# Moving the first batch's token turns and router products between two blocks of an attention and mixture-of-experts kernel

## The reference

```
x = x + LN(attention(LN(x)))
x = x + LN(ffn(LN(x)))

attention: qkv = x @ w_qkv, 16 heads of 8 channels
  scores = q k^T / sqrt(8), causal mask, + head_scale * q_proj * k_proj
  out = softmax(scores) v @ w_out
ffn: logits = x @ router_w^T over 7 experts; top 2 by value, softmax of the two
  expert(x) = (silu(x @ w_gate) * (x @ w_up)) @ w_down, hidden width 512
  out = sum over the two chosen experts of weight * expert(x) + shared expert(x)
```

## Time and profile before

| | us |
|---|---|
| median of 3 runs | 510.47 |
| the profiled execution | 510.59 |
| span of the profile, first to last instruction | 508.9 |
| PE busy | 421.5 (83%) |
| DVE busy | 337.0 (66%) |
| ACT busy | 247.2 (49%) |
| POOL busy | 185.3 (36%) |

### The profile page before, as it was taken

The page is one execution under the profiler, slowest core; times in us unless marked ns, Lnnn a source line. Parts: engine busy times, 40 slices in busy tenths (PEclk is TensorE's granted clock), DMA queues, the critical chain, the costliest instruction groups (busy, mean ns, idle before and its releaser), DMA issues. The chain is left out here.

```text
span 508.9 us, 10326 instructions
## 1 busy us (share of the span) xinstructions
PE 421.5 (83%) x3468; PEld 237.3 (47%) x3468; DVE 337.0 (66%) x1133; ACT 247.2 (49%) x432; POOL 185.3 (36%) x341
## 2 busy tenths in 40 slices
PE   1745999999999999999999688979699989899600
PEld 0421122333333333333333455646699989899600
DVE  2975988999898989898938636794133222233267
ACT  1430147777777777787878167342222123123230
POOL 9100021423323232415141125345256655664322
PEclk9995559999999999999999679999799989999955
DMA  3066364202011010000000081004267756667152
GB/s 109 1 166 172 91 194 127 64 3 56 11 32 34 9 58 2 3 3 3 3 2 1 0 246 44 3 0 149 83 225 212 210 164 211 205 221 229 64 166 83
DMA packets 43944, 46.55 MB, mean 91 GB/s; under 512 B 5683, under 2 KB 32692, under 8 KB 43892
## 3 DMA queue, kind: packets, MB, share of 16 engines
q1 hardware_dynamic: 41460, 40.91, 27.0%
q0 software_dynamic: 2432, 4.99, 3.5%
HBM read 34.80 MB, written 10.88 MB: 90 GB/s over the span
## 5 line engine op out<-in xcount | busy, mean ns | idle before, releaser
L590 ACT ACTIVATE probs<-banks 128x1024 f32<-128x1024 f32 (+2 forms) x192 | 151.7, 809 | 37.4 <-PE banks L437 35.5
L425 PE MATMUL banks<-k_st,q_st 48*128 48x512 bf16 (+3 forms) x384 | 121.8, 358 | 14.0 <-DMA k_st<-k_rows 11.5
L344 POOL TENSOR_SCALAR_AFFINE_SELECT probs<-probs 128x256 f32<-128x256 f32 x128 | 52.2, 408 | 141.9 <-ACT probs L590 141.1
L455 PE MATMUL banks<-probs,v_pad 128*32 128x256 f32 (+1 forms) x1280 | 97.0, 375 | 1.9 <-ACT o_cols L601 1.0
L437 PE MATMUL banks<-q_st,k_st 51*128 51x512 bf16 (+3 forms) x384 | 93.4, 335 | 3.5 <-DVE mx_part L716 1.3
L716 DVE TENSOR_REDUCE mx_part<-banks 128x1 f32<-128x512 f32 x128 | 77.6, 679 | 5.7 <-PE banks L425 5.7
L1463 DVE TENSOR_TENSOR hidden<-banks,gate 128x512 f32<-128x512 f32 x38 | 26.3, 692 | 65.0 <-ACT gate L1231 25.9
L722 DVE CUSTOM_DVE_ANT_0 scratch<-banks,mask_qk,mx_part 128x384 f32<-128x384 f32 (+3 forms) x128 | 63.9, 548 | 5.5 <-PE banks L425 5.5
L722 DVE CUSTOM_DVE_ANT_0 scratch<-banks,mask_qk 128x512 f32<-128x512 f32 (+3 forms) x128 | 56.2, 486 | 13.7 <-PE banks L425 12.5
L425 PEld LDWEIGHTS banks<-k_st,q_st 48*128 48x128 bf16 x384 | 32.1, 94 | 58.1 <-DVE mx L722 20.1
L437 PEld LDWEIGHTS banks<-q_st,k_st 51*128 51x128 bf16 x384 | 23.5, 94 | 69.9 <-issue 39.1
(11 more groups left out here) (190 smaller groups left out, 460.3 us busy)
## 6 DMA issues: line engine op xcount, KB each, us to landing
w_g<-in_w_gate SPq DMA_DIRECT2D x38, 256.0 KB
w_u<-in_w_up SPq DMA_DIRECT2D x38, 256.0 KB
q_rows<-parts SPq DMA_DIRECT2D x24, 128.0 KB, 2.4
k_rows<-parts SPq DMA_DIRECT2D x24, 128.0 KB, 2.4
q_st<-q_rows SPq DMA_DIRECT2D x32, 96.0 KB, 2.3
k_st<-k_rows SPq DMA_DIRECT2D x32, 96.0 KB, 2.3
w_d<-in_w_down SPq DMA_DIRECT2D x8, 256.0 KB, 4.8
back<-results SPq DMA_DIRECT2D x8, 256.0 KB, 5.0
```

Source lines behind the costliest of these rows:

```text
L344: nc.gpsimd.affine_select(out=part, in_=part, compare_op=ALU.is_ge, fill=0.0, base=0, pattern=[[0, 2], [1, P]], channel_multiplier=-1).the ...
L425: nc.tensor.matmul(max_bank[m % RING][:, 0:width], q_st[r][rows, c, p, (i % CH) * P:(i % CH + 1) * P], k_st[r][rows, kc, p, 0:width], star ...
L455: last = nc.tensor.matmul(o_bank[h * HQ:(h + 1) * HQ, lo:hi], v_pad[:, n, j, h, :], probs[unit % PROBS][:, h, lo:hi], start=(x in FIRST_UN ...
L590: return nc.scalar.activation(probs[unit % PROBS][:, 2 * p:2 * p + 2, first:BANK], slot_pair[p].rearrange("p (a t) -> p a t", a=2)[:, :, 0 ...
```

## The change

NEWTON goes from 4 to 3. In the last group the projection of the first batch is issued behind unit 3 instead of unit 4. The first block's token turns, x2_t copies, router products and logits copy are gone (`first_turn_tokens`, `first_route` and their banks and semaphore). DVE inverts the first half of the last group's sums ahead of writing x2 and the second half right behind it. In the second block PE turns chunk 0 behind its attention turns, then projects, then turns chunk 1; DVE copies both at the head of its list, ahead of its wait for the projection. The router products of chunks 0 and 1 follow shared_up of chunk 0. One copy takes all logits.

```diff
--- before.py
+++ after.py
@@ -43,7 +43,7 @@
 MINUS_ONES = float(np.array([0xBF80BF80], np.uint32).view(np.float32)[0])
 EPS = 1e-5
 RSQRT_BITS = float(0x5F3759DF)
-NEWTON = 4
+NEWTON = 3
 E, HID = 7, 512
 NE = E + 1
 HT = HID // P
@@ -171,7 +171,7 @@
         slot_bank = [[bank(RING + 2 * i + a) for a in range(2)] for i in range(2)]
         slot_pair = [bank(RING + 2 * i, 2) for i in range(2)]
         o_bank = bank(7)
-        first_proj_bank, first_x2_bank, first_lg_bank = [bank(2), bank(0)], [bank(1), bank(2)], bank(0)
+        first_proj_bank = [bank(2), bank(0)]
 
         x_loaded = [sem(f"x_loaded{b}") for b in range(B)]
         weights_loaded = sem("weights_loaded")
@@ -217,7 +217,6 @@
         first_turned = sem("first_turned")
         first_attn_t_ready = sem("first_attn_t_ready")
         first_projected = sem("first_projected")
-        first_logits_done = sem("first_logits_done")
         post_var_ready = sem("post_var_ready")
         post_std_ready = sem("post_std_ready")
         x2_ready = sem("x2_ready")
@@ -489,21 +488,6 @@
                                                 start=True, stop=True)
                     last.then_inc(first_projected, 1)
 
-            def first_turn_tokens():
-                for q in range(2):
-                    pe.wait_ge(x2_ready, q + 1)
-                    for j in range(CH):
-                        last = nc.tensor.transpose(first_x2_bank[q][:, j * P:(j + 1) * P],
-                                                   x2[:, q * CH + j, :], ident[:, :])
-                    last.then_inc(x2_transposed, 1)
-
-            def first_route():
-                pe.wait_ge(x2_t_ready, 2)
-                for t in range(KT):
-                    last = nc.tensor.matmul(first_lg_bank[:, t * 8:t * 8 + E], x2_t[:, t, :], router_sb[:, :],
-                                            start=True, stop=True)
-                last.then_inc(first_logits_done, 1)
-
             pe.wait_ge(parts_ready, 4)
             pe.wait_ge(v_stored, 4)
             pe.wait_ge(consts_ready, 3)
@@ -539,7 +523,7 @@
                             weighted_values(unit // UNITS, unit % UNITS, 1 - p)
                     if n == GROUPS - 1 and x == 2:
                         first_turn_attn()
-                    if n == GROUPS - 1 and x == 4:
+                    if n == GROUPS - 1 and x == 3:
                         first_project()
             weighted_values(GROUPS - 1, UNITS - 2, 1)
             weighted_values(GROUPS - 1, UNITS - 1, 0)
@@ -549,8 +533,6 @@
                 for a in range(2):
                     last = turn_outputs(GROUPS - 1, 1, 2 * p + a, slot_bank[p][a][:, BANK - P:BANK])
                 last.then_inc(outs_turned, 1)
-            first_turn_tokens()
-            first_route()
 
 
         @block.scalar
@@ -774,20 +756,12 @@
                                     ).then_inc(vector_steps, step.one())
             dve.wait_ge(vector_steps, step.now())
             layer_norm(lambda t: x_sb[:, t, :])
+            invert_sums(GROUPS - 1, 0)
             for t in range(KT):
                 last = nc.vector.tensor_scalar(x2[:, t, :], x_sb[:, t, :], mean_var[:, t, 0:1],
                                                rstd[:, t:t + 1], ALU.subtract, ALU.mult)
                 if t % CH == CH - 1:
                     last.then_inc(x2_ready, 1)
-            for q in range(2):
-                dve.wait_ge(x2_transposed, q + 1)
-                nc.vector.tensor_copy(x2_t[:, q * CH:(q + 1) * CH, :].rearrange("p t c -> p (t c)"),
-                                      first_x2_bank[q]).then_inc(x2_t_ready, 1)
-            dve.wait_ge(first_logits_done, 1)
-            nc.vector.tensor_copy(logits[:, 0:KT, 0:E],
-                                  first_lg_bank[:, 0:KT * 8].rearrange("p (t e) -> p t e", e=8)[:, :, 0:E]
-                                  ).then_inc(vector_steps, step.one())
-            invert_sums(GROUPS - 1, 0)
             invert_sums(GROUPS - 1, 1)
 
         front.close()
@@ -1028,16 +1002,11 @@
                         last = nc.tensor.transpose(at_bank[half][:, j * P:(j + 1) * P],
                                                    attn[:, 1, half * CH + j, :], ident[:, :])
                     last.then_inc(attn_transposed, 1)
-                for half in range(2):
-                    pe.wait_ge(attn_t_ready, half + 1)
-                    for j in range(CH):
-                        last = nc.tensor.matmul(pr_bank[half][:, j * P:(j + 1) * P],
-                                                attn_t[:, half, j * P:(j + 1) * P], w_out_sb[:, :],
-                                                start=True, stop=True)
-                    last.then_inc(projected, 1)
 
                 def turn_tokens(q):
                     pe.wait_ge(x2_ready, q + 1)
+                    if q >= 2:
+                        pe.wait_ge(x2_t_ready, q - 1)
                     for j in range(CH):
                         last = nc.tensor.transpose(xt_bank[q % 2][:, j * P:(j + 1) * P],
                                                    x2[:, q * CH + j, :], ident[:, :])
@@ -1078,9 +1047,21 @@
                                 start=(t == 0), stop=(t == HT - 1))
                     last.then_inc(s_down_done, 1)
 
+                turn_tokens(0)
+                for half in range(2):
+                    pe.wait_ge(attn_t_ready, half + 1)
+                    for j in range(CH):
+                        last = nc.tensor.matmul(pr_bank[half][:, j * P:(j + 1) * P],
+                                                attn_t[:, half, j * P:(j + 1) * P], w_out_sb[:, :],
+                                                start=True, stop=True)
+                    last.then_inc(projected, 1)
+                turn_tokens(1)
                 pe.wait_ge(shared_loaded, 16 * 3)
                 pe.wait_ge(proj_ready, 2)
+                pe.wait_ge(x2_t_ready, 2)
                 shared_up(0, range(HT))
+                route(0)
+                route(1)
                 shared_up(1, [0])
                 shared_down(0)
                 shared_up(1, [1])
@@ -1281,6 +1262,10 @@
                     done()
 
 
+                for q in range(QC):
+                    dve.wait_ge(x2_transposed, q + 1)
+                    nc.vector.tensor_copy(x2_t[:, q * CH:(q + 1) * CH, :].rearrange("p t c -> p (t c)"),
+                                          xt_bank[q]).then_inc(x2_t_ready, 1)
                 dve.wait_ge(proj_ready, 2)
                 layer_norm(lambda t: proj[:, t - KT, :], KT, KT, post_var_ready, post_std_ready, 1)
                 for t in range(KT, NT):
@@ -1297,9 +1282,9 @@
                                                    rstd[:, t:t + 1], ALU.subtract, ALU.mult)
                     if t % CH == CH - 1:
                         last.then_inc(x2_ready, 1)
-                dve.wait_ge(logits_done, QC)
-                nc.vector.tensor_copy(logits[:, KT:, 0:E],
-                                      lg_bank.rearrange("p (t e) -> p t e", e=8)[:, KT:, 0:E]
+                dve.wait_ge(logits_done, CHUNKS)
+                nc.vector.tensor_copy(logits[:, :, 0:E],
+                                      lg_bank.rearrange("p (t e) -> p t e", e=8)[:, :, 0:E]
                                       ).then_inc(steps, step.one())
                 done()
                 for t in range(NT):
```

## The result

Over 20 executions each the changed kernel took 508.77 us (503.87 to 514.23) and the kernel before 513.88 (509.88 to 520.78). The ratio is 0.9904, 95% interval 0.9876 to 0.9931: 4.9 us faster, between 3.5 and 6.4. Forecast were 504.3 us, in a range of 499.3 to 506.8, from a base of 510.47. The time lies outside the range. As a ratio the forecast was 0.988, inside the interval.

The account below looks back on a forecast made before the run. The first block's end was taken as bound by the last group's reciprocals, queued on DVE behind other work. Terms -7.7 + 0.9 + 0.6 + 0.05 = -6.2 us from a 510.47 us base gave 504.3 us, range 499.3 to 506.8.

Parts of the forecast that it names:

- The base: Whole kernel: time before the change taken as 510.47 us, the median of three runs; the profiled execution took 510.59.
- own range: Whole time: the forecast's range without its rivals, 503.2 to 505.3 us around 504.3.
- The first block, -7.7: End of the first block: POOL's last multiply ends at 285.5 us instead of 293.21.
- ACT would be next at the end: First block's end: second reciprocal waits for ACT's last copy at 284.67 us, so about 0.5 us stays unused.
- Rival A: First block: the hole in front of unit 4 costs the full 2.05 us, giving 506.1 us; chance 0.13.
- The second block's head, +0.9: Second block ahead of the shared products: moved turns and copies cost 0.9 us, bounds 0 and +1.8.
- The bound of 0 on the good side: Second block's head: with the full clock the way takes 5.0 us, but the loads hold it, so 0.
- Router products, +0.6: Second block: first batch's routing products cost 1.95 us, less 1.16 of PE idle and 0.2 of overlap.
- forecast of 6.2: Whole kernel: the summed gain, -6.2 us, with ends -7.1 and -5.3.
- B: After 351.5 us: ACT's hold has a time of its own and swallows the gain, 510.5 us; chance 0.11.
- C: Behind the shared products: ACT's hold disappears, another -4.9 us, giving 499.4 us; chance 0.08.
- D: Expert loop: shifted streams bring further ACT holds of 4.9 us; from three on 519.0 us, slower; chance 0.06.

Follow-up runs that it names:

- move: Kernel before with only the token turns, copies and router products moved to the second block (four Newton steps, projection behind unit 4, both reciprocals behind x2); ratio 0.9971.
- unit4: Changed kernel with the first projection back behind unit 4; 510.34 us in one execution.
- start_after: Changed kernel with added PE products that nothing reads, to keep the clock up in the first block; 525.58 us, ratio 1.0195 to the kernel before.
- start_hole: Changed kernel with added unread PE products in the first block and the first batch's router products in PE's hole in chunk 0; 524.49 us, ratio 1.0236.
- the ahead ones: Changed kernel with 4 or 6 row gathers issued ahead instead of 8; ratios 0.9897 and 0.9881 to the kernel before.
- ahead4: Changed kernel with 4 row gathers issued ahead instead of 8; median 515.67 us against 514.53, ratio 0.9897.
- again: The kernel before, unchanged, once more; median 511.38 us, ratio 0.999.
- after_third: Changed kernel, unchanged, once more; 510.35 us against 513.66 for the kernel before, ratio 0.9823.

## Why the prediction was right and wrong

**The base.** This is the step that failed: "the median of the three runs is 0.12 lower, 510.47, so 504.3 us". The profiled execution had the early rise of the clock, and the median of the three lies beside it. Twenty executions of that kernel gave 513.88, other sets 513.4, 514.5, 513.7, and another chip 495.7. The range was built from rivals in the kernel and had no term for the base; from 510.47 to 513.88 are 3.4 of the 4.5 us by which the forecast missed. The other 1.1 is gain that did not come: 5.1 us by the medians against 6.2. (The own range, 503.2 to 505.3, should read 503.4 to 505.2 by its own ends; that changes nothing.) Two stretches of unchanged code scatter by as much as the base was off: the one up to the marker, with two positions of the clock's rise and 3.8 us between the two traces, and the expert loop, 115.5 to 119.1 us on the slower chips. That the clock is the cause of the first was not shown, since the attempt to force it failed; what moves the second is open.

**The first block, -7.7.** Measured -7.7 (29.6 to 21.9). The share of the parts: 5.7 for the move; 1.4 for the Newton steps and the order of the reciprocals together (from 23.9 in move to 22.5 in unit4); 0.5 for the projection behind unit 3 (unit4). The reciprocals without the move gave 1.0, since another tail then ends the block. The forecast that ACT would be next at the end, and that 0.5 us of DVE's gain would lie unused, is in the rows: DVE waits 0.73 us for ACT. ACT itself was later by 288.15 + 0.45 - 267.43 = 21.17 against 284.37 - 263.59 = 20.78: 0.4, where 0.3 was taken. Rival A fell.

**The second block's head, +0.9.** The way to the first shared product was 5.0, 4.8 and 5.8 us in the three runs of the changed kernel (6.1 before) and 5.9 to 7.5 in the six runs where the clock was low at the seam. The term was mis-sized: at most +1.4, in the changed kernel's own runs -0.3 to -1.3. The forecast took it that the clock would fall as before; with the block ending soon after PE's last turns it did not in 7 of the 13 traces that have the moved products, two of them with PE kept going by added turns. The other half of the error is a misreading: the row at 299.67 names the loads as the releaser, and the sum took them as landing at 6.10 us. ACT's copy had ended 0.1 us before, and PE's own row of that place in the trace before names it:

```profile
299.70 1.10 PE L1061 MATMUL banks<-x_t,s_w_g 128*128 128x512 f32 x2 [0.78 <-ACT proj L1168]
```

Where the copies are done early, the loads turn out to land anywhere from 4.8 to 6.2 us after the block's start. The bound of 0 on the good side excluded a gain that came.

**Router products, +0.6.** Measured +0.5.

**What was not in the sum.** The clock fell once more behind the router products of chunks 2 and 3 and cost 1.1 us there ("behind" 7.2 instead of 6.1): in 8 of the 13 traces with the moved products, start_after, start_hole and the ahead ones among them, and in none of 5 with the products in the first block. Of the changed kernel's own three traces two had it. Whether the change makes it likelier or this was chance stays open. The Trainium skill, "TensorE: Matmul & The Clock Gate", Part 1, says that the moments of the clock's changes are not tied to the kernel's start; the runs agree, the changed kernel's clock rose at 75.1 in one trace and at 90.2 us in another, which is much further apart than the page gives for the first rise.

**The balance.** By the traces the changed kernel should be 7.7 us faster in the first block, and a third of a microsecond slower from the second block's start to the second shared down products (32.8, 32.6 and 32.5 against 32.4 and 32.2). The measured ratio gives 3.5 to 6.4 us, on the other chip 4.4 to 8.4 of 495.7. At 513.9 us at least 1 us of the 7.4 was not found. The expert loop, whose code is the same, took 116.5 to 118.1 us in the five traces with the products in the first block and 115.5 to 119.1 in the eight with them moved (the slower chips, 8 gathers ahead), so a difference of this size can be neither located there nor excluded. That the forecast of 6.2 lies nearer to the measured gain than these 7.4 do is luck: the head was priced 1.2 us too dear, and that covered part of what was not found.

**Rivals B, C, D.** ACT's hold behind the shared products neither swallowed the gain nor went away: 9.12 and 9.24 us. It is a matter of the gathers issued ahead (ahead4, one trace) and of the chip (0.04 us on the other one, with 8 ahead). D counted two holds, at 360.62 and 408.72, and took the whole 3.29 us of the second. The trace has more: up to 480 us ten further waits of ACT in the expert loop end like that, nine in the changed kernel's trace, seven in again, five in after_third. They did not multiply with the change; on the fourth chip no trace has one.

## What to carry to other kernels

Before a forecast in absolute time, ask how many executions the base stands on, and whether the profiled one is typical: a stretch ahead of the change that differs between two traces of the same code gives the width of the base, and belongs into the range. When work is taken out of the tail of a block, price the new tail by the engine that is late next; that number held to 0.1 us. Work that is moved costs its own time less the holes at its new place; look for the hole first (11.92 to 11.42 us by moving two lines).

## What the runs showed of the hardware that was not expected

- The same kernel took 513 to 515 us on three chips and 495.7 us on a fourth. The expert loop accounts for most of it: from ACT's last shared copy to the last hidden product it took 104.2 us in the changed kernel there and 115.5 to 119.1 elsewhere, and the hold of 5.0 us ahead of it was absent. There ACT's waits for turned rows were at most 1.30 us and named PE; elsewhere 2 to 10 of ACT's waits in the loop ended by nothing that the profile shows, most of them 2.4 to 4.2 us long.
- In traces with the hold, ACT is released about 5 us after the recorded end of the products that it waits for, while POOL issues nine gathers. With five gathers it is released on time, and on the fourth chip with nine as well. Recorded ends of products are modelled; what PE really did in these 5 us was not settled.
- A low clock in the last group itself costs too: start_after, with the first block's tail of the changed kernel, ended 23.6 us from its marker instead of 21.9, its clock having been low from 283 to 290 us, across the marker at 286.4.
